# Value product of a pair in one step, and a row's scores split around its step's first transposes

## The reference

```python
x = _layernorm(x + _L0_gnn_ref(x, L0_gnn_W, L0_gnn_a, adj))       # gated sums over neighbours
x = _layernorm(x + _L1_gnn_ref(x, adj, Wh, bh, Wo, bo, gamma, beta))
x = _layernorm(x + _L2_gnn_ref(x, adj, L2_gnn_weight, L2_gnn_a))
x = _layernorm(x + _L3_gnn_ref(x, adj, L3_gnn_W, L3_gnn_a))

# L1: four heads, then a second attention over their concatenation, both of this form
scores = where(mask, h @ h.T, -1e16); out = softmax(scores) @ h + b
# L2 and L3: additive scores, slope 0.01 and 0.2
e = leaky(left[:, None] + right[None, :]); out = softmax(where(mask, e, NEG)) @ h
```

## Time and profile before

| | us |
|---|---|
| median of 3 runs | 6281.87 (6273.06 to 6285.5) |
| the profiled execution, its own time | 6281.5 |
| its span, first to last instruction | 6279.7 |
| TensorE busy | 5612.5 (89%) |
| VectorE busy | 4379.2 (70%) |
| ScalarE busy | 3844.2 (61%) |
| GpSimd busy | 1784.7 (28%) |
| mean granted TensorE clock | 0.956 |

### The profile page before, as it was taken

How to read it: one execution, slowest core, us unless ns; L and a number is a source line. 1 busy time by engine, 2 the same in 40 slices (tenths; PEclk the granted TensorE clock), 3 DMA queues, 4 the chain that set the end, 5 groups by cost and what they waited for, 6 DMA issues and landing times.

```text
span 6279.7 us, 163342 instructions
## 1 busy us (share of the span) xinstructions
PE 5612.5 (89%) x52064; PEld 4569.8 (73%) x52064; DVE 4379.2 (70%) x7705; ACT 3844.2 (61%) x5701; POOL 1784.7 (28%) x1659
## 2 busy tenths in 40 slices
PE   7679998998989889998989989898899989899866
PEld 4368777886768777786778867787777867788755
DVE  4856567767776677767777677766777677776765
ACT  1046557666576666667576666767576675766665
POOL 0100015014240424205250242404242052402455
PEclk9889999999999999999999999999999999999988
DMA  4200000000000000000000000000000000000000
GB/s 142 59 11 2 2 5 2 2 2 10 4 2 2 2 12 2 2 2 3 11 2 2 2 10 4 2 2 2 12 2 2 2 3 11 2 2 2 8 1 5
DMA packets 98616, 55.36 MB, mean 9 GB/s; under 512 B 88800, under 2 KB 92128, under 8 KB 97760
## 3 DMA queue, kind: packets, MB, share of 16 engines
q1 hardware_dynamic: 59872, 34.45, 2.0%
q10 hardware_dynamic: 37888, 9.97, 0.7%
HBM read 35.49 MB, written 8.91 MB: 7 GB/s over the span
## 4 chain that ended last, share of the span: by engine, by line
PE 69%; issue 9%; DVE 7%; ACT 5%; DVEq 3%; POOLq 1%; POOL 1%; ACTq 0%; DMA 0%; SPq 0%
PE tp L917 22%; PE po L937 20%; PE pss L905 9%; PE pss L906 9%; DVEq L259 3%; DVE rows L1193 2%; PE px L866 2%; DVE pt L1205 2%; PE px L925 2%; ACT pss L1077 1%; ACT rows L1097 1%; PE px L862 1%; POOLq L259 1%; PE px L880 1%; PE px L872 1%
## 5 line engine op out<-in xcount | busy, mean ns | idle before, releaser
L917 PE MATMUL tp<-ident,rows 128*128 128x128 f32 x14336 | 2003.1, 282 | 165.0 <-DVE pt L1205 116.4
L1205 DVE COPY pt<-tp 128x512 f32<-128x512 f32 x2048 | 1339.1, 687 | 1071.8 <-PE tp L917 1060.0
L917 PEld LDWEIGHTS tp<-ident,rows 128*128 128x128 f32 x14336 | 1630.5, 144 | 498.5 <-issue 433.3
L1097 ACT ACTIVATE rows<-rows,nm 128x2048 f32<-128x2048 f32 x896 | 1795.3, 2004 | 287.1 <-DVE nm L1193 278.7
L937 PE MATMUL po<-pt,hn 128*64 128x128 f32 x28672 | 1808.6, 280 | 35.0 <-ACT ot L1058 33.5
L937 PEld LDWEIGHTS po<-pt,hn 128*64 128x64 f32 x28672 | 1593.7, 140 | 194.6 <-issue 194.4
L1050 ACT COPY pt<-tp 128x512 f32<-128x512 f32 x1536 | 840.9, 589 | 722.1 <-PE tp L917 715.6
L748 POOL TENSOR_TENSOR rows<-sr,mask 128x2048 f32<-128x2048 f32 x256 | 1046.8, 4092 | 290.2 <-PE tp L917 282.1
L905 PE MATMUL pss<-ha 128*128 128x512 f32 x2560 | 1072.8, 419 | 15.0 <-issue 12.7
L906 PE MATMUL pss<-ha,hb 128*128 128x512 f32 x2560 | 1018.7, 398 | 0.0
L1193 DVE CUSTOM_DVE_ANT_0 rows<-pss,mask,nm 128x1024 f32<-128x1024 f32 x640 | 821.8, 1284 | 210.4 <-issue 207.6
(11 more groups left out here) (105 smaller groups left out, 3500.8 us busy)
## 6 DMA issues: line engine op xcount, KB each, us to landing
adjb<-in_adj SPq DMA_DIRECT2D x32, 512.0 KB, 4.6
xin<-x SPq DMA_DIRECT2D x34, 128.0 KB, 2.3
xb<-in_x ACTq DMA_DIRECT2D x16, 256.0 KB, 3.3
x<-t ACTq DMA_DIRECT2D x16, 256.0 KB, 2.7
xb<-x SPq DMA_DIRECT2D x8, 512.0 KB, 5.0
out<-xb SPq DMA_DIRECT2D x32, 128.0 KB, 1.9
xtp<-in_xt SPq DMA_DIRECT2D x12, 256.0 KB, 6.9
ab<-in_a ACTq DMA_DIRECT2D x16, 64.0 KB, 3.1
```

What stands on the lines that cost most here:

```text
L917: last = nc.tensor.transpose(tp[q % 2][:, r * P:(r + 1) * P], rows[:, row.slot, jb * P:(jb + 1) * P], ident[:])
L1097: nc.scalar.activation(rows[:, row.slot, :], rows[:, row.slot, :], ACT.Exp, scale=-1.0, bias=nm[:, row.place, 1:2], accum_out=rs[:, row.pl ...
L1205: nc.vector.tensor_copy(pt[:, CH * q:CH * (q + 1), row.k % SLOTS, :], tp[q % 2][:].rearrange("p (j n) -> p j n", n=P)).then_inc(pt_dve, 1)
```

## The change

Two things change in the order of work; no instruction is added or taken out.

- `dot_products` now does one half. Half 0 stays at the head of the step, half 1 comes behind the transposes of quarters 0 and 1 of the row s - 2 (and for a step whose row has no rows to turn, behind its tasks). The semaphores that each half waits for and gives are the same.
- `sum_values` of a pair does both halves in the step s - 3, that is in the even step, behind the second half of the scores. ScalarE's `take_sums` moves to the end of that same step. The step s - 4, the odd one, has no value product.

```diff
-            def dot_products(row):
+            def dot_products(row, half):
                 i, rows_t = PROJ[row.unit], slice(row.t * P, (row.t + 1) * P)
-                if row.t == 0:
+                if row.t == 0 and half == 0:
                     wait(h2_c)
-                for half in range(2):
-                    if row.k:
-                        wait(read_c, read_c.n + 2 * (row.k - 1) + half + 1)
+                if row.k:
+                    wait(read_c, read_c.n + 2 * (row.k - 1) + half + 1)
...
                     if row and row.gat:
-                        dot_products(row)
+                        dot_products(row, 0)
                     for task in segment.tasks.get(s, ()):
                         run_task(*task)
...
                         turn(turned, 0)
                         turn(turned, 1)
+                    if row and row.gat:
+                        dot_products(row, 1)
                     if segment.odd(s - 3):
                         sum_values(segment.odd(s - 3), 0)
-                    if segment.odd(s - 4):
-                        sum_values(segment.odd(s - 4), 1)
+                        sum_values(segment.odd(s - 3), 1)
...
                     copy_tile(turned, 3)
-                    if segment.odd(s - 4):
-                        take_sums(segment.odd(s - 4))
+                    if segment.odd(s - 3):
+                        take_sums(segment.odd(s - 3))
```

More of the change, by code:

```diff
@@ L893, in run_task @@
                     px_used(sr_c)
-            def dot_products(row):
+            def dot_products(row, half):
                 i, rows_t = PROJ[row.unit], slice(row.t * P, (row.t + 1) * P)
-                if row.t == 0:
+                if row.t == 0 and half == 0:
                     wait(h2_c)
-                for half in range(2):
-                    if row.k:
-                        wait(read_c, read_c.n + 2 * (row.k - 1) + half + 1)
[L902 to L907, removed]
+                if row.k:
+                    wait(read_c, read_c.n + 2 * (row.k - 1) + half + 1)
+                for c in range(half * NC // 2, (half + 1) * NC // 2):
+                    cols = slice(c * BANK, (c + 1) * BANK)
+                    moving = ha[i][:, cols]
+                    nc.tensor.matmul(pss[:, cols], ha[i][:, rows_t], moving, start=True, stop=False)
+                    last = nc.tensor.matmul(pss[:, cols], hb[i][:, rows_t], moving, start=False, stop=True)
+                last.then_inc(scores_ready, 1)
             def turn(row, q):
```

## The result

The changed kernel takes 6835.34 us (median of 4, 6826.91 to 6837.85) against 6283.68 us before: a ratio of 1.0879, interval 1.086 to 1.0898, 552 us slower. The direction was forecast, the size was not: 6630 us with a range from 6390 to 6760.

What follows compares the result with a forecast made beforehand. TensorE was taken to bound dot-product stretches, VectorE's row of work additive ones. Terms -32 + 224 + 82 + 5 + 70 = +349 us on 6281.5 us gave 6630 us, range 6390 to 6760.

Steps and rivals of the forecast that it cites:

- Two kernels by stage, and TensorE's own time: TensorE bounds dot-product stretches, VectorE additive ones; TensorE's work per dot-product pair falls from 11.41 to 11.32 us, -32 us.
- The stall in dot-product pairs: Once per dot-product pair, TensorE's transposes in the even step wait 0.70 us for VectorE's later copies, +224 us.
- Additive pairs: Even additive steps: VectorE's copies wait behind 1.74 us more value product; 1.3 us per clean pair, 82 us plus 5.
- Steps with tasks: Steps carrying extra tasks: VectorE tasks lengthen odd dot-product steps, even-step tasks hide better; net +70 us, bounds -140 and +200.
- The clock: Additive odd steps leave TensorE idle, the clock drops to 1.2 GHz and the doubled value product slows: +87 us, chance 0.12.
- Rival 3: Additive stretches: lower TensorE clock adds 2.4 us to the value product in half of 72 steps; 6717 us, chance 0.12.
- Rivals 1, 2 and 4: No stall, faster, 6230 us, 0.09; only the dot-product stall costs, 6473 us, 0.15; all cancels within 0.2%, 0.04.
- Rival 1: Dot-product pairs: no stall if VectorE's quarter 3 copy ends by 1.45 us into the even step; 6230 us, chance 0.09.

Runs made afterwards that it cites:

- the version with early copies: Changed kernel, additive value product in two steps; in odd dot-product steps ScalarE does half-step tasks and all four copies before its exponential: 6410.4 us, ratio 1.0206.

## Why the prediction was wrong

- **Two kernels by stage, and TensorE's own time.** Right in kind, a little dear in size. The value product as one block was 3.64 us and is 3.65; the odd step's blocks were 3.74 and are 3.61. Four score products take 1.01 to 1.02, as priced; it is the eight transposes between score blocks that take 0.79 and not 0.85. A pair without the stall is 11.11 us, as the version with early copies shows, and not 11.32.
- **The stall in dot-product pairs.** Right in mechanism and nearly in size: the wait for VectorE's copy of quarters 2 and 3, 0.79 us where I had 0.70. That the pair came to 11.90 where I had 12.0 is two errors that cancel in part, 0.21 too much for the blocks and 0.09 too little for the stall. Moving these copies to ScalarE took the stall away.
- **Additive pairs.** Right: 87 us forecast, 99 measured by taking it back.
- **Steps with tasks.** This is the step that failed: +70 us, bounds -140 and +200. With 157 us of clean loss and 99 of additive, about 296 us are left of the 552. I counted only VectorE's work ahead of its copies, and said of tasks in even steps that they are hidden better. I left out two things. The first is ScalarE's queue: a copy of `px` in the second part of a step stands behind the exponential. The change takes its cover, the half value product ahead of xt and four of the eight score products ahead of h, and makes the exponential itself only 0.3 us later. Before, TensorE's idle time ahead of h was 8.1 us in all, and I took no row for it; it was a wait just covered, and is 72.6. (The wait of r for VectorE I had, with 28 x 1.55 = 43 us of which I took half; its idle time went from 6.2 to 59.9.) Moving xt half a step gave 82 us back in steps 8 to 31 alone. The second is TensorE's own order: a task at the head of a step now stands ahead of the second half of the scores, so that its work and its waits delay VectorE and the exponential (second half 4.29 us behind the first in step 24, before 1.53). The turning back's wait did go, and by more than I said (111.9 to 27.5 us), but the idle time ahead of hn grew by as much in other steps (93.3 to 175.8).
- **The clock.** Rival 3 had it, with 0.12, and in the wrong place. It was priced for additive odd steps; there the joined product made it worse too (steps 40 to 47 from 8.3 us a pass at the lower level to 14.6), but steps 16 to 31 (2.0 to 13.7) and 80 to 87 (none to 10.5) were dot-product steps at or near full clock before, which I held to be safe. It rode on the waits that I had missed, and filling some of these gave 109 us. I had also written that nothing shows longer waits than 0.55 us in additive steps. That was a wrong reading: in the trace of before TensorE is idle for 1.67 us ahead of 1050.94 and 0.91 ahead of 1053.69, just before the throttled product of the earlier trace rows.
- **Rivals 1, 2 and 4** fell. (Rival 1's limit of 1.45 us leaves out the 0.15 of delay behind a copy and should be 1.30; that changes nothing here.) Part of what I held against rival 1, that VectorE's idle time lies in front of its copies, is confirmed; but my first theory after the result, that only both parts together stall, fell in turn: each alone costs, the joining mostly in clean steps through ScalarE's copy of quarter 0, the splitting in steps with tasks.

The two remedies overlap: 130 us by moving tasks, 109 by the filling, 325 by the early copies don't add up, since a wait that is gone also brings its clock back. In the whole kernel 391 us are waits and 162 slower work; how the 296 us divide is not settled. Nor are steps 8 to 15, with +64 us in the changed kernel, which no run took apart; 26 us of it are longer waits of hn for VectorE's subtraction in steps 9 and 10.

## What to carry to other kernels

When a piece of work is moved later, follow every queue in which something stands behind it, tasks of other stages too, and look at what now stands between it and its old place: a queue that works in order hands every wait in between on to it. A wait near zero in the trace is not a free wait; ask what covers it and whether the change takes the cover. And before work is gathered into one of two alternating steps, lay the other engines' full work beside the short step: what is hidden in two equal steps need not be in a short and a long one.

## What the runs showed of the hardware

- A wait of some 2 us cost more behind it: with 18 transposes put into it, step 20 ran at a granted clock of 1.00 instead of 0.84 and was 1.56 us shorter. Added work that nobody reads made the kernel 109 us faster.
- Splitting the scores cost nothing in whole steps (11.42 us for a pair with two entries from transposes into scores more, 11.41 before). Each entry costs 0.10 us in the score block (1.02 for four products, 0.92 without an entry), also where both sides are 128 x 128; but eight transposes take 0.79 us between two score blocks, 0.85 after and 0.96 ahead of the value product. The Trainium skill's page "TensorEngine Tiling (Array Packing)", section "Key Properties", has it that a change of the tiling mode drains the engine. The trace agrees in that transposes are dearer next to the value product's tile shape, and that from scores to it the start is 0.33 us later (2067.78 to 2068.11 in the changed kernel), where it is 0.23 between score products.
